# Transposing the next tile's gate weights one step later in a two-layer graph and expert network

## The reference

```
x = x + W . concat(mean over edges of feat[src] * w, feat) + b        # graph layer 0
x = x + sum over the 2 best of 8 experts: c_e * (relu(xn W1_e + b1_e) W2_e + b2_e)   # hidden 512
x = x + h W1 + sqrt(sum over edges of w * h[src]**2) W2 + biases, h = relu(xn Wp + bp)
x = x + sum over the 2 best of 8 experts: c_e * (gelu(xn W1_e + b1_e) W2_e + b2_e)   # hidden 256
```

## Time and profile before

| | |
|---|---|
| median of three timed runs | 2748.9 us (2745.66 to 2751.58) |
| the profiled execution | 2746.08 us |
| its span, first to last instruction | 2744.2 us |
| busy: PE, DVE, ACT, POOL | 2265.4, 1857.9, 1296.2, 1710.3 us |
| layer 0, about | up to 1575 us |
| layer 1, about | from 1575 us |

### The profile page before, as it was taken

How to read it: one execution, slowest core, us unless ns; L and a number is a source line. 1 busy time by engine, 2 the same in 40 slices (tenths; PEclk the granted TensorE clock), 3 DMA queues, 4 the chain that set the end, 5 groups by cost and what they waited for, 6 DMA issues and landing times.

```text
span 2744.2 us, 45870 instructions
## 1 busy us (share of the span) xinstructions
PE 2265.4 (83%) x16513; PEld 1420.9 (52%) x16513; DVE 1857.9 (68%) x4929; ACT 1296.2 (47%) x2221; POOL 1710.3 (62%) x1678
## 2 busy tenths in 40 slices
PE   0137999999999999999999734588878778988987
PEld 0124555555555555555558634444444444567876
DVE  8576777778778777787776644355555555667775
ACT  4023455454454554544556601244334444566667
POOL 3677666575575665764430077777777777777760
PEclk9999999999999999999999955699999999999999
DMA  5733333343333333432220032122222222222220
GB/s 208 253 104 110 102 107 103 97 120 88 98 111 92 106 103 97 118 93 82 72 64 21 32 108 62 51 63 70 69 57 63 70 70 63 63 67 71 71 61 11
DMA packets 116317, 237.92 MB, mean 87 GB/s; under 512 B 30434, under 2 KB 70364, under 8 KB 115572
## 3 DMA queue, kind: packets, MB, share of 16 engines
q0 software_dynamic: 66560, 163.68, 21.3%
q1 hardware_dynamic: 49524, 71.26, 7.7%
HBM read 209.16 MB, written 25.67 MB: 86 GB/s over the span
## 4 chain that ended last, share of the span: by engine, by line
PE 47%; POOL 24%; DVE 12%; issue 11%; ACT 4%; DMA 2%; DVEq 0%; POOLq 0%; ACTq 0%; SPq 0%
POOL ring L625 23%; PE psY L757 18%; PE psH L721 17%; PE psM L821 4%; PE psE L703 2%; DVE hsc L1334 1%; PE psE L711 1%; DVE hid L1328 1%; DMA ring<-table,src_s 1%; PE psM L773 1%; PE psE L731 1%; PE psE L705 1%; PE psM L781 1%; ACT L1506 1%; DVE wbuf L1074 1%
## 5 line engine op out<-in xcount | busy, mean ns | idle before, releaser
L625 POOL DMA_INDIRECT ring<-table,src_s x1664 | 1680.7, 1010 | 902.4 <-issue 624.1
L721 PE MATMUL psH<-xnT,wbuf 128*128 128x512 f16 (+2 forms) x4320 | 909.9, 348 | 8.3 <-ACT hid L1517 8.3
L757 PE MATMUL psY<-hsc,wbuf 128*128 128x512 f16 (+2 forms) x4320 | 902.9, 345 | 11.2 <-DVE hsc L1334 6.2
L1517 ACT ACTIVATE hid<-psH,b,scl 128x512 f32<-128x512 f32 (+2 forms) x720 | 503.4, 699 | 761.1 <-PE psH L721 757.8
L1328 DVE TENSOR_TENSOR hid<-hid,cS 128x512 f32<-128x512 f32 (+2 forms) x720 | 427.7, 594 | 452.0 <-ACT cS L1524 310.1
L757 PEld LDWEIGHTS psY<-hsc,wbuf 128*128 128x128 f16 x4320 | 415.5, 99 | 391.4 <-issue 23.6
L721 PEld LDWEIGHTS psH<-xnT,wbuf 128*128 128x128 f16 x4320 | 406.1, 102 | 300.8 <-issue 21.1
L1334 DVE TENSOR_TENSOR hsc<-hid,hsc 128x512 f16<-128x512 f32 (+2 forms) x720 | 423.1, 588 | 0.4 <-ACT hsc L1531 0.3
L711 PE MATMUL psE<-ohbuf,ring 128*128 128x40 f32 x1664 | 251.1, 306 | 186.7 <-DMA ring<-table,src_s 186.5
L1531 ACT ACTIVATE hsc<-hid 128x512 f16<-128x512 f32 (+2 forms) x720 | 392.0, 544 | 27.1 <-DVE hid L1328 26.1
L711 PEld LDWEIGHTS psE<-ohbuf,ring 128*128 128x128 f32 x1664 | 238.3, 219 | 233.4 <-DMA ring<-table,src_s 227.9
(11 more groups left out here) (163 smaller groups left out, 1938.6 us busy)
## 6 DMA issues: line engine op xcount, KB each, us to landing
ring<-table,src_s POOLq DMA_INDIRECT x1664, 2.5
wbuf<-w_in SPq DMA_DIRECT2D x2, 4096.0 KB, 20.7
wbuf<-x_in SPq DMA_DIRECT2D x7, 896.0 KB, 12.7
table<-ring SPq DMA_DIRECT2D x7, 896.0 KB, 3.6
feat<-table SPq DMA_DIRECT2D x11, 512.0 KB, 4.0
xin<-x_in SPq DMA_DIRECT2D x11, 512.0 KB, 3.9
x_d<-x SPq DMA_DIRECT2D x11, 512.0 KB, 3.5
wbuf<-w_in SPq DMA_DIRECT2D x2, 2048.0 KB, 11.2
```

What stands on the lines that cost most here:

```text
L625: pool.indirect_dma_start(out=l.ring[:, g % l.R, k, :], out_offset=None, in_=l.table, in_offset=bass.IndirectOffsetOnAxis(ap=src_s[:, c:c ...
L721: last = mm(psH[n % 2][:, 0:l.TT[t]], l.w1(e, i, k, c), x[:, j, k, 0:l.TT[t]], start=(k == 0 and m == 0), stop=(k == KD - 1 and m == 2))
L757: last = mm(psY[d][:, 0:l.TT[t]], l.w2(e, i, c, d), h[:, j, 0:l.TT[t]], start=False, stop=(n == l.M - 1 and m == 2))
L1517: f(hid[(l.M * t + n) % HB][:, 0:l.TT[t]], psH[n % 2][:, 0:l.TT[t]], (ACT.Relu, ACT.Gelu)[l.i], scale=l.un_up, bias=l.b1[:, n // l.HC, n % ...
```

## The change

PE's `weights_transposed(l, t + 1)` moves from the end of step `at_comb` to step `at_comb + 1`, between that step's `up` and its `down`. `at_comb + 1` is M - 2 in both layers, the step whose `up` is chunk 0 of the next tile and whose last matmul is the spread for expert 0 of the next tile. The wait for ACT's copy (`comb_ready`) leaves `down` and moves to the head of that spread, where a wait for the PSUM bank (`window_added` or `spread_copied`) already stands. Nothing changes on the other engines, and no instruction but the wait's place is added or removed. The start of each layer (tile 0) keeps its order.

```diff
             def spread_weights(l, t, e):
 
                 x = NX * t + e
+                if t and e == 0:
+                    pe.wait_ge(l.comb_ready, t + 1)
                 added, copied = l.spread_after[x]
                 wait(pe, l.window_added, added)
                 wait(pe, l.spread_copied, copied)
@@
                 for d in range(KD):
                     for m, (i, j) in enumerate(PARTS):
-                        if d == 0 and m == 1 and at[1] + 2 == l.M and at[0] < l.NT - 1:
-                            pe.wait_ge(l.comb_ready, at[0] + 2)
@@
                         elif not last:
                             up(l, t + 1, n + 2 - l.M)
+                        if n == l.at_comb + 1 and not last:
+                            weights_transposed(l, t + 1)
                         if n:
                             down(l, t, n - 1, (t, n))
@@
                             logits(l, t + 1)
-                        if n == l.at_comb:
-                            weights_transposed(l, t + 1)
```

## The result

The changed kernel takes **2729.44 us** (median of four runs, 2729.02 to 2732.18) beside 2747.28 (four runs, 2745.05 to 2751.58): ratio 0.994, interval 0.9922 to 0.9959, or 16.5 us less (11 to 21); the two medians are 17.8 apart. The forecast was 2732, the range 2727 to 2740. The profiled execution took 2729.02 with a span of 2727.2, 17.0 less than before's 2744.2.

The account below looks back on a forecast made before the run. PE was taken to bound the first layer, GpSimd's gather most of the second. Gains of 13.4 + 2.0 = 15.4 us gave 2730.7 from the profiled execution, 2733.5 from the median; forecast 2732 us, range 2727 to 2740.

Parts of the forecast that it names:

- main term: First layer's full tiles: the up-product fills PE's wait for DVE ahead of the transposes, nine tiles x 1.28 = 11.5 us.
- The short tiles: First layer's last tiles: gains of 0.95, 0.66 and 0.33 us, each the lesser of wait and up-product.
- What comes earlier: Behind the spread, ACT's cS copy and DVE's scaling come 1.28 us earlier; DVE still fits, 0.36 us idle left.
- Rival B: First layer: VectorE takes PE's place as bound, the gain returns as down-product waits on hsc; price 13.4 us, chance 0.09.
- The copy and the pair of waits: At the spread: ACT's copy and two waits in a row cost 0; upper ends 1 us and 4 us.
- The cover: Full tiles: the copy ends 0.5 us before PE reaches the spread, thanks to the down-product between.
- The second layer: Nothing gained while GpSimd sets the pace; the tail behind the last gathers gives 2.0 us.
- The gather as a metronome: Second layer: GpSimd's 832 gathers take 1088 us from first to last issue, which PE cannot push.
- rival D: Second layer: the gather takes longer; 0.03 us more per issue stretches it by 25 us, to 2757; chance 0.04.
- the cap: Second layer's tail: the last gather's landing limits the gain at PE's 1.21 us wait to 1.05 us.
- rival C: Second layer's tail: narrow products slowed by the clock behind long waits run faster, 1.5 us in all, 2730; chance 0.06.
- The sum: Whole kernel: 13.4 us from the first layer plus 2.0 from the second, 15.4 us gained.

Follow-up runs that it names:

- wait alone: Changed kernel with the transposes back at the end of step at_comb, so only the wait for ACT's copy moves to the spread: 2748.49 us, ratio 1.0005 to before.
- transposes alone: Changed kernel with the wait for ACT's copy kept ahead of the down-product's second matmul, so only the transposes move: 2740.47 us, ratio 0.9978 to before.
- DVE later: Changed kernel with two extra memsets on DVE ahead of its release of the gate weights: 2741.44 us, ratio 0.9972 to the kernel before.
- second layer alone: Changed kernel with the old order restored in the first layer, the change kept in the second: 2742.8 us, ratio 0.9986 to the kernel before.
- pairs everywhere: Changed kernel with the wait for the copy ahead of every spread behind each layer's first tile: 2731.71 us, ratio 0.9948 to the kernel before.
- later copy: Changed kernel with two more ACT copies of the same size ahead of the real one: 2737.59 us, ratio 0.9963 to the kernel before.

## Why the prediction was right

**The bound and the main term.** "The gain of one tile is the lesser of the wait and the up-product": 109.39 - 108.10 = 1.29 in full tiles, where 1.28 was taken. The kernels that tell it from mere reordering are the wait alone (109.39), the transposes alone (108.75) and DVE later (108.88). That wait (1.28 or 1.29) and up-product (1.29) are equal within 0.01 is luck, which the rows showed beforehand; it is why nothing was left of the wait, and also why nothing is in hand.

**The short tiles.** 0.95, 0.66 and 0.33 were read as such.

**What comes earlier.** DVE's 0.36 us of idle time left: 0.35. Rival B did not come. PE's waits on hsc are 3.1 us in five times from 300 to 1528, as they were from 300 to 1545 before; the 3.7 in six of the list above takes in one more at its end, which the kernel before has too, behind 1545.

**The copy and the pair of waits.** Both at zero in full tiles. The cover was put at 0.5 and is 0.44. The Trainium skill, "Perfetto Trace Analysis", section "Identifying Dependency Chains", says that an instruction which waits on several engines may get a semaphore instruction ahead of it: the counts agree (+29, +232). The end at which that would cost 0.30 us each did not show in the period, 108.10 with one pair as with eight. In the 256-column tiles, where the cover was put at about nil, nothing showed either: of the 248 spreads of the changed kernel none shows an idle time ahead of it.

**The second layer.** The gather as a metronome held: between 1086 and 1093 us from first to last in eight profiled executions, the one before and seven others, with no sign of rival D. The tail gave 2.0 in this execution, of which 1.0 by the cap that was read off the last groups; how far it can be relied on stands under rival C below.

**The sum against the time.** Predicted for the profiled execution 2730.7, measured 2729.02, so 1.7 too few. The terms of the change don't fill this. 16.9 us at the first gather stand against the 13.4 of the sum, and 3.0 of these lie ahead of the first transposes that could gain: 339.01 in the earlier trace rows, 335.99 after. The cause is in tile 0, before the change has moved anything. PE's timeline there, first of the kernel before and then of the changed one:

```profile
276.82 0.21 PE L703 MATMUL psE<-ohbuf,ring 128*128 128x80 f16 x1 [2.62 <-DMA ring<-table,src_s]
...
277.50 2.73 PE L721 MATMUL psH<-xnT,wbuf 128*128 128x512 f16 x6
```

```profile
275.44 0.21 PE L703 MATMUL psE<-ohbuf,ring 128*128 128x80 f16 x1 [1.59 <-DMA ring<-table,src_s]
...
275.99 1.46 PE L721 MATMUL psH<-xnT,wbuf 128*128 128x512 f16 x6
```

A gather landed 1.4 us later, and behind the longer wait the products ran at the lower clock (granted 0.50 from 277.4 to 280.3, against 1.00 from 275.9 to 278.8 in the change). That it is chance and not the change is shown by runs of either order. The wait alone and the second layer alone have the old order here, and their transposes at the second tile start at 444.76 and 445.15, not at 448.40; "DVE later" has the new order and a product of 2.73 at 276.52, and its first transposes start at 338.99. Without the 3.0 the first gather comes 13.9 us earlier, against 13.4. The stretch of the gathers gave 1.9 of this back, within its spread of 7. So of the 17.0 us in the spans 13.9 and 2.0 are the change's, 0.5 more than the sum, and 3.0 - 1.9 = 1.1 is luck.

**Rival C was right in its cause, but its gain did not come.** The slow products behind the last transposes went (1.32 to 0.82), but they came behind the ones before (0.82 to 1.49), where the wait is now shorter. Granted clock and busy time of those stretches, in order: the kernel before, the changed one, and the one with pairs everywhere, which has the changed order too:

```profile
2689.00:2693.00 4.00, 4.00 (x39) 3.58 (x40) 2.22 (x6) 2.47 (x6) 0.00 (x0) 1.00 0.00 0
2720.30:2723.30 3.00, 2.97 (x24) 2.36 (x25) 1.42 (x4) 1.77 (x6) 0.00 (x0) 0.63 0.01 3
```

```profile
2673.00:2677.00 4.00, 4.00 (x23) 2.95 (x24) 2.27 (x6) 2.39 (x6) 0.00 (x0) 0.57 0.00 0
2705.40:2708.40 3.00, 3.00 (x37) 2.79 (x38) 1.84 (x6) 1.79 (x7) 0.00 (x0) 1.00 0.02 5
```

```profile
2671.00:2675.00 4.00, 4.00 (x25) 2.95 (x23) 2.06 (x6) 2.32 (x6) 0.00 (x0) 0.61 0.00 0
2703.20:2706.20 3.00, 3.00 (x19) 2.43 (x20) 1.56 (x5) 1.83 (x6) 0.00 (x0) 0.53 0.03 8
```

0.57 means mostly the lower level of 1.2 GHz. From the last transposes to the end took 23.9 us before, 21.8 in the change and 23.2 with pairs everywhere; 0.33 of the first difference is the change's, 1.7 the clock's. Between the last two transposes PE paid 1.7 to the clock (31.4 us before, 32.4 after, where 0.66 less was due). So a slow stretch is worth some 1.5 us of this tail. The second layer alone, which has the changed order here, repeats the changed kernel (0.58, then 1.00; 78.5 us from the last gather to the end). With pairs everywhere there are two slow stretches, and from the last gather to the end it takes 80.7 us, no less than before. So two of three executions of this order show the 2.0 of the tail, and the third shows none of it: there the clock takes as much as the change gives. What decides it was not settled. Behind the wait of the last transposes but one the granted clock stayed at 1.00 where the wait was 3.01, 3.00 (wait alone) and 2.86 (DVE later) and fell where it was 2.35, 2.35 and 2.34, but in the run with the later copy it stayed at 1.00 behind 2.34 as well.

## What to carry to other kernels

Where an engine is full and one short wait stands in its row every tile, look for an instruction behind the wait that needs nothing of what is waited for: the gain is the lesser of the two durations, and it can be read from two rows before anything is built. Move the next wait with it, to its last possible place, for the work that now lies behind the moved step is the cover of the step that follows; transposes alone gave half. Then check that what you gained reaches the end: in this kernel only the tiles ahead of the GpSimd-bound stretch did for sure, and those behind its last gathers in two executions of three.

## What was not expected of the hardware

- **The same kernel is 13 to 14% slower on some chips.** Kernel before: 2747 and 2748 us on two chips, 3139 and 3107 on two others. The gather's issues last the same (938/946/1951 ns beside 940/946/1925), but there are many stops that the profile puts down to "remote". Waits and a timeline row of the changed kernel on such a chip:

```profile
ACT hid L1517 <- remote: 350.1, 105, 21.7
POOL ring L625 <- remote: 221.7, 108, 5.9
```

```profile
530.25 0.78 ACT L1517 ACTIVATE hid<-psH,b,scl 128x512 f32<-128x512 f32 x1 [5.10 <-remote]
```

The list of the same kernel's waits on the first chip has no such line among its longest. The instructions of ACT and DVE keep their durations (777 and 691 ns for the full-tile forms of L1517 and L1328 on both), and the mean granted clock is 0.893 where it was 0.941. Why is open. The change is worth the same share on both, as far as the intervals tell (0.9939 and 0.994).
- **A pair of waits on PE is an instruction that costs nothing where the wait is long fulfilled**: 232 of them, period of full tiles unchanged at 108.10.
- **One profiled execution carries some 3 us of chance** ahead of the part that is compared (a DMA's landing and products at the lower clock), and the tail another 1.5. A period over seven equal tiles was repeatable to 0.01 us (109.39 in three executions, 108.10 in two), when medians of ten runs had intervals of 5 us.
